# Masking the second-pass probabilities of key tile 3 on GpSimd instead of TensorE

## The reference

```python
h = relu(layernorm(x))
q, k, v = heads(h @ Wq + bq), heads(h @ Wk + bk), heads(h @ Wv + bv)
scores = einsum('bhqd,bhkd->bhqk', q, k) * scale
scores = where(adj[:, None] == 0, -inf, scores)
attn = softmax(scores, axis=-1)
x = x + einsum('bhqk,bhkd->bhqd', attn, v) @ Wo + bo
```

## Time and profile before

| | |
|---|---|
| median of 3 runs | 1721.32 us (1720.43 to 1723.81) |
| profiled execution, its own time | 1723.0 us |
| its span, first to last instruction | 1721.1 us |
| TensorE busy | 1661.3 us, 97% |
| VectorE busy | 1533.7 us, 89% |
| ScalarE busy | 1475.2 us, 86% |
| GpSimd busy | 146.1 us, 8% |
| mean granted clock of TensorE | 0.988 of full speed |

### The profile page before, as it was taken

One profiled execution on the slowest core, in us unless ns is written; L12 is line 12 of the kernel. 1 busy time (PEld: TensorE's weight loads), 2 busy tenths in 40 slices (PEclk: granted clock), 3 DMA queues, 4 the chain that ended last, 5 costly groups with the idle time before them and its releaser, 6 DMA issues.

```text
span 1721.1 us, 27544 instructions
## 1 busy us (share of the span) xinstructions
PE 1661.3 (97%) x8001; PEld 1037.7 (60%) x8001; DVE 1533.7 (89%) x3659; ACT 1475.2 (86%) x3497; POOL 146.1 (8%) x199
## 2 busy tenths in 40 slices
PE   6789999999999999999999999999999999999998
PEld 4546665665666666666665666666666666666643
DVE  5799998999989899898999989899898999989885
ACT  3699898888988989889898988989888888988975
POOL 0001100011010010100001000011100011010010
PEclk9799999999999999999999999999999999999989
DMA  6334343433433344343333433344343333433320
GB/s 189 97 90 110 99 108 83 117 90 110 112 99 111 82 117 111 99 106 87 115 91 108 115 92 113 85 117 112 99 105 85 113 93 109 113 97 100 88 76 25
DMA packets 117164, 175.15 MB, mean 102 GB/s; under 512 B 30860, under 2 KB 32920, under 8 KB 117016
## 3 DMA queue, kind: packets, MB, share of 16 engines
q1 hardware_dynamic: 112344, 171.56, 37.0%
q10 hardware_dynamic: 4672, 1.84, 0.5%
HBM read 54.79 MB, written 16.78 MB: 42 GB/s over the span
## 4 chain that ended last, share of the span: by engine, by line
PE 78%; DVE 15%; issue 3%; ACT 2%; ACTq 1%; DMA 0%; SPq 0%; DVEq 0%
PE ps L775 14%; PE psO L809 13%; PE psP L679 12%; PE psP L680 11%; PE ps L789 11%; PE psP L681 11%; DVE ps L572 5%; DVE probs L579 4%; PE ps L792 3%; PE ps L726 1%; DVE x_tile L491 1%; ACT ps L412 1%; DVE stats L483 1%; DVE neg_max L572 1%; DVE oT_lo L592 1%
## 5 line engine op out<-in xcount | busy, mean ns | idle before, releaser
L572 DVE CUSTOM_DVE_ANT_0 ps<-ps,bias_q 128x512 f32<-128x512 f32 x1024 | 708.7, 694 | 136.2 <-PE ps L775 126.8
L412 ACT ACTIVATE ps<-ps,neg_max 128x512 f32<-128x512 f32 x1024 | 686.7, 671 | 101.4 <-DVE neg_max L572 83.3
L448 ACT ACTIVATE probs<-ps 128x512 f32<-128x512 f32 x1024 | 621.3, 607 | 74.1 <-PE ps L792 69.7
L579 DVE SCALAR_TENSOR_TENSOR probs<-bias_k,probs 128x512 f32<-128x512 bf16 x768 | 552.4, 720 | 8.1 <-ACT probs L448 8.0
L775 PE MATMUL ps<-k_stack,q_stack 96*128 96x512 f32 x1024 | 451.7, 441 | 19.2 <-ACT ps L412 13.9
L789 PE MATMUL ps<-q_stack,k_stack 98*128 98x512 f32 x1024 | 410.7, 401 | 3.7 <-ACT probs L448 3.5
L775 PEld LDWEIGHTS ps<-k_stack,q_stack 96*128 96x128 f32 x1024 | 194.6, 190 | 276.2 <-ACT ps L412 135.5
L809 PE MATMUL psO<-probs,v_sb 128*32 128x512 f32 x2048 | 275.0, 609 | 2.1 <-DVE oT_lo L592 0.9
L789 PEld LDWEIGHTS ps<-q_stack,k_stack 98*128 98x128 f32 x1024 | 195.4, 191 | 40.5 <-ACT probs L448 15.7
L412 ACT ACTIVATION_READ_ACCUMULATOR ps<-ps,neg_max 128x1 f32 x1024 | 217.9, 213 | 0.0
L572 DVE DVE_READ_ACCUMULATOR2_ANT neg_max<- 128x1 f32 x1024 | 144.0, 141 | 0.0
(11 more groups left out here) (75 smaller groups left out, 1930.6 us busy)
## 6 DMA issues: line engine op xcount, KB each, us to landing
q_stack<-part_hi SPq DMA_DIRECT2D x512, 64.0 KB, 2.0
k_stack<-part_hi SPq DMA_DIRECT2D x504, 64.0 KB, 2.0
x_tile<-in_x_dram SPq DMA_DIRECT2D x64, 256.0 KB, 2.9
y_tile<-in_x_dram SPq DMA_DIRECT2D x64, 256.0 KB, 2.9
adj_tile<-in_adj_dram SPq DMA_DIRECT2D x64, 256.0 KB, 3.0
q_stack<-part_lo SPq DMA_DIRECT2D x256, 64.0 KB, 2.0
k_stack<-part_lo SPq DMA_DIRECT2D x252, 64.0 KB, 2.0
out_dram<-y_tile SPq DMA_DIRECT2D x62, 256.0 KB, 2.1
```

What stands on the lines that cost most here:

```text
L412: nc.scalar.activation(item, item, ACT.Exp, scale=-1.0, bias=neg_max[:, g % 2, col:col + 1], accum_out=exp_sum[:, col:col + 1]).then_inc(e ...
L448: nc.scalar.activation(probs[:, n % P_RING, :], ps2[:, n % 2, :], ACT.Exp, scale=SCALE).then_inc(exp2_done, 1)
L572: nc.vector.tensor_tensor_reduce(bank1(("s", u)), bank1(("s", u)), bias_q[:, qt, :], -SCALE, 3.0e38, ALU.add, ALU.min, neg_max[:, g % 2, c ...
L579: nc.vector.scalar_tensor_tensor(out=probs[:, n % P_RING, :], in0=bias_k[:, n % 16 // 4, :], scalar=-MASKED, in1=probs[:, n % P_RING, :], ...
```

## The change

The masks of pass 2 are divided by key tile. VectorE masks key tiles 0, 1 and 2 of every head group with the same instruction as before (12 of each 16 tiles in a row, then 4 not); GpSimd masks key tile 3 (n % 16 in 12 to 15) by an integer product of the probability's bits with a 0/1 tile `keep_k`; TensorE's mask matmul is gone. `bias_k` holds three key tiles instead of four; ScalarE writes key tile 3 from PSUM as `keep_k` (int32, 1 + bias / 2^100). The second turn of the mask moves from slot 61 to slot 62, and its move to SBUF is now two instructions, of which the second waits for all products of the graph before. GpSimd's small work is placed in slots among the products.

```diff
-VECTOR_MASKED = (0, 1, 2, 4, 5, 6)
+GPSIMD_KEY_TILES, VECTOR_KEY_TILES = (3,), (0, 1, 2)
...
-         24: [("c", 2, -1)], 40: [("c", 3, -1)], 53: [("m", 0, 0)], 56: [("c", 0, 0)], 61: [("m", 1, 0)]}
+         24: [("c", 2, -1)], 40: [("c", 3, -1)], 53: [("m", 0, 0)], 56: [("c", 0, 0)], 62: [("m", 1, 0)]}
...
+            def mask(b, n):
+                kt = n % 16 // 4
+                if n < 16 and n % 4 == 0:
+                    pool.wait_ge(m_done, due(2 * b + kt // 2 + 1))
+                pool.wait_ge(exp2_done, due(64 * b + n + 1))
+                tile = probs[:, n % P_RING, :].bitcast(I32)
+                nc.gpsimd.tensor_tensor(tile, tile, keep_k[:, GPSIMD_KEY_TILES.index(kt), :], ALU.mult).then_inc(gpsimd_masked, 1)
+
             def step(k, parity):
...
+                for u in range(SLOTS):
+                    if k > 0 and u == 5: form_rstd(k, 2)
+                    if k > 0 and u == 10: form_rstd(k, 3)
+                    if u == 12 and k - 2 != LAST: add_bo(k - 2, 3)
+                    b, n = pass2(k, u)
+                    if have(b) and n % 16 // 4 in GPSIMD_KEY_TILES:
+                        mask(b, n)
+                    if u == 8 and k - 2 != LAST: add_bo(k - 2, 2)
+                    if u in (43, 44): form_rstd(k + 1, u - 43)
+                    if u in (49, 50): add_bo(k - 1, u - 49)
+                    if u in (52, 53) and k - 1 == LAST: add_bo(LAST, u - 50)
...
+                            turned = bank1((kind, n, rel)).bitcast(BF16)
+                            act.wait_ge(vector_masked, due(VECTOR_ALL * (k - 1) + masked_before(48 + 8 * n + 8, VECTOR_KEY_TILES)))
+                            if n == 0:
+                                nc.scalar.activation(bias_k[:, 0:2, :], turned.rearrange("p (t q) -> p t q", q=S), ACT.Identity).then_inc(m_done, 1)
+                            else:
+                                nc.scalar.activation(bias_k[:, 2, :], turned[:, 0:S], ACT.Identity).then_inc(bias_k_done, 1)
+                                act.wait_ge(gpsimd_masked, due(GPSIMD_ALL * k))
+                                nc.scalar.activation(keep_k[:, 0, :], turned[:, S:2 * S], ACT.Identity,
+                                                     scale=-1.0 / MASKED, bias=1.0).then_inc(m_done, 1)
...
-                    if have(b) and n % 8 in VECTOR_MASKED:
+                    if have(b) and n % 16 // 4 in VECTOR_KEY_TILES:
...
-                        last = nc.tensor.matmul(ps2[:, n % 2, :], k_stack[:, g, j, P * kt:P * kt + P], q_stack[:, g, j, :],
-                                                start=True, stop=(n % 8 in VECTOR_MASKED))
-                        if n % 8 not in VECTOR_MASKED:
-                            last = nc.tensor.matmul(ps2[:, n % 2, :], ident_b[:], bias_k[:, kt, :], start=False, stop=True)
-                        last.then_inc(scores2, 1)
+                        nc.tensor.matmul(ps2[:, n % 2, :], k_stack[:, g, j, P * kt:P * kt + P], q_stack[:, g, j, :],
+                                         start=True, stop=True).then_inc(scores2, 1)
...
-                        pe.wait_ge(probs_masked, due(MASKED_ALL * b + masked_before(4 * n + 4)))
+                        if kt in VECTOR_KEY_TILES:
+                            pe.wait_ge(vector_masked, due(VECTOR_ALL * b + masked_before(4 * n + 4, VECTOR_KEY_TILES)))
+                        else:
+                            pe.wait_ge(gpsimd_masked, due(GPSIMD_ALL * b + masked_before(4 * n + 4, GPSIMD_KEY_TILES)))
```

38 lines of the change are left out of this document (13 added, 25 removed).

## The result

The changed kernel takes 1761.28 us (median of 4 runs, 1757.05 to 1762.83) against 1722.57 for the kernel before on the same chip (4 runs, 1720.43 to 1725.91): ratio 1.0224, 95% interval 1.0207 to 1.024. The forecast was 1707 us, the range ended at 1738: wrong in direction and outside the range. The profiled execution has a span of 1760.8 us, 39.7 more than before.

The account below looks back on a forecast made before the run. It took TensorE's list to bound the kernel nearly everywhere, VectorE close behind: 58.9 us gross, less 43.5 (2.9 in each of fifteen blocks) and 1.3 once, gains 14.1 us. Forecast 1707 us, range 1672 to 1738.

Parts of the forecast that it names:

- gross gain: TensorE loses 256 mask matmuls at 0.23 us each: 58.9 us in all, 3.7 us per block.
- bunching: Twelve mask-heavy slots in a row, then four light; in slots 14 to 21 VectorE has 12.96 us against TensorE's 11.80.
- slots 2-13 (1st group): GpSimd's products and small work delay slot 14's PV product and normalisation L491: 0.9 us per block, bounds 0.3 and 2.5.
- slots 14-21: Eight VectorE masks instead of six put it 1.2 us behind, mostly absorbed: 0.3 us charged, bounds 0 and 1.2.
- borders / slots 38-45: GpSimd's products meet VectorE's masks where light slots begin, half of three borders hit: 0.3 us per block.
- slots 46-53: VectorE's 12.90 us plus 1.2 us of masks; 13.4 us taken, bounds 12.5 and 14.1: 0.9 us charged.
- slots 54-1 (turn): ScalarE's split mask move, one slot later, delays attention output and output projection: 0.5 us per block, bounds 0 and 1.
- tail, once: At the very end the last product stands between the last exponential and last PV product: 1.3 us once.
- VectorE as the bound: Rival: eight products per block each cost a mask or L491 1.2 us, VectorE needs 104.3 us; 1732 us, chance 0.15.
- The slow integer product: Rival: GpSimd's product takes over about 1.6 us; at 2.0 us 1738, at 2.6 us near 1840; chance 0.15.
- the gain is kept: Rival: VectorE's light slots absorb the charges, only about 0.8 us per block is lost: 1676 us, chance 0.25.
- Masks of 1.2 to 1.8 us at the borders only: Sign of being right: VectorE's masks stretched only at borders; stretched masks inside groups would show the forecast wrong.

Follow-up runs that it names:

- e12: The kernel before the change with GpSimd's bias additions cut to one column (the rest of the bias left out): 1700.7 us, ratio 0.9879.
- e9: e6 with the masks divided in the old order, GpSimd on every fourth tile (3 and 7 of 8), some mask tiles wrong: 1661.59 us, ratio 0.9646.
- e3: The changed kernel with the second turn of the mask back in slot 61: 1739.9 us, ratio 1.0103.
- e4: The changed kernel with GpSimd's bias additions on one column instead of 512: 1719.92 us, ratio 0.9983.
- e7: The changed kernel with the turn in slot 61 and the bias additions of slots 49 and 50 moved to 57 and 58: 1713.29 us, ratio 0.995.
- e2: The changed kernel with GpSimd's products on one column instead of 512: 1727.39 us, ratio 1.0044.
- e1: The kernel before with masks divided by key tile, key tile 3 staying on TensorE, no product on GpSimd: 1756.76 us, ratio 1.0201.
- e6: The changed kernel with GpSimd's products and bias additions on one column and the turn back in slot 61: 1690.72 us, ratio 0.9822.
- e5: The changed kernel with both GpSimd's products and its bias additions on one column: 1706.7 us, ratio 0.9918.

## Why the prediction was wrong, step by step

The gross gain was right for the quiet stretches: 0.23 us per matmul, 5.88 us per four slots as forecast. But even without locks, bunching and moved turn only 39 of the 58.9 us arrive (e12 to e9). The charges against the full gain were 2.9 us per block and measured 6.0 (each is the mean stretch after, less the mean stretch before and its full gain):

```
                      forecast  measured
slots 2-13 (1st group)   0.9      1.12
slots 14-21              0.3      0.44
borders / slots 38-45    0.3      0.51
slots 46-53              0.9      1.95
slots 54-1 (turn)        0.5      1.95 (1.37 of it the turn, e3)
tail, once               1.3      8.7 (5.0 longer, and the 3.7 of its own gain gone)
```

The 3.1 us more in each of 15 blocks and the 7.4 more in the tail are 54 us, the whole miss from 1707 to 1761.

**The step that failed first: slots 46 to 53.** The prediction added 1.2 us of masks to VectorE's 12.90 and took 13.4, "nearer to VectorE's row because nothing was absorbed before". The mean is 14.68, above even the upper bound. Bunching explains 0.4 of the 1.95 us: with the additions short or elsewhere the stretch takes 13.10 (e4 to e7). What failed is the term for the addition's lock, which it held to be "in these numbers" already. Its row (rows 5) has one addition in the stretch, and the other 2.1 us ahead. It did not ask where the new products would push GpSimd's old work: into the stretch, where the first addition makes VectorE late and the second meets the normalisation, in 11 of 15 blocks. e12 has this lock at 0.46 us per block, e2 at 0.57, the changed kernel at 1.58. A lock is not a constant that can be carried from one schedule to the next; it depends on what is met. How much VectorE's missing slack adds by itself is not separated; between e12 and e2 it is 0.1 us, though e1, with bunched masks and its additions placed as before, has some 0.9 (14.04 less 13.10, an estimate).

**The second: the turn.** The prediction charged 0.5 us, bounds 0 and 1, from ScalarE's own time for the moves. What counted was their place in an in-order list: the moves wait for a turn that TensorE starts only after its PV product, and the exponential and the high part behind them wait as well. The stretch 62-1 became 1.31 us longer in two blocks of three. Nor was it foreseen that in the others the granted clock falls as well (+1.58 us). e3 and e6 put the whole at 16 to 21 us; 7.5 were charged. That the wait lowers the clock is not shown by a run of its own. It is argued from what comes just ahead, and from e6 and e7, which have neither the wait nor a lowered clock there.

**The third: bunching.** It was seen (12.96 against 11.80 us in slots 14 to 21) and "most of it is absorbed" was right for those slots (0.16 us, e9 to e6). It costs 29 us (e9 to e6) in places that had no term for it or too small a one: slots 2 to 9 (0.60 us), 38 to 45 (0.46), 46 to 53 (0.48) and the tail (5.75 once).

**Right in size by luck: the first group.** The charge was 0.9 us and measured 1.12, but the prediction let the PV product of slot 14 wait for GpSimd's chain. It waits in none of the 15 blocks: the last product is done 0.7 to 2.3 us ahead of it. TensorE's hole in slots 10 to 13 is a wait of 0.6 us per block for the exponential L421, against 0.2 us in e5. And the working's line that L522 at 412.07 is not stretched shows nothing, since no 128x512 instruction of GpSimd was under way then; that it is not stretched is shown by other rows (below).

**The rivals.** The second, VectorE as the bound (1732 us), is nearest to the case that came, though not as it was built and 29 us too low: its price was eight products each meeting a mask. In fact 54 of the 768 masks and 18 of the 62 normalisations take over 0.8 us, all of them in the first group, in slots 46 to 53 and in the last block; the full-length instructions cost 9.4 us in the tail besides (92.21 to 82.76 in e5). It had a chance of 0.15, too low for an engine at 12.90 of 12.97 us. The slow integer product had as much and was wrong: 1.31 us. That the gain is kept did not come true in any run: with short products and additions, the old order and the old turn, 39 of 58.9 us are left of it.

Of the signs named ahead, these came: 5.88 us, products of 1.27 to 1.71 us, VectorE without idle time and TensorE with holes in slots 46 to 53. "Masks of 1.2 to 1.8 us at the borders only" did not: 1217.44 and 1226.73 lie inside. The Trainium skill's rule ("SBUF — State Buffer", SBUF: two separate sides), by which a lock is held for a whole instruction, agrees with the stretched rows shown here (the mask of 1226.73 runs on until 0.55 us behind the addition's end). What a lock costs the kernel, and that was the error, had to come from the schedule.

## What to carry to other kernels

When a change puts new work into an engine's list, look at where it pushes the old work of that list, and what the old work will meet there: in slots 46 to 53 the same two additions cost 0.46 us per block before, 0.57 with the products cut short and 1.58 behind full ones, when they met the normalisation. Look at how masks, or whatever is shared out, follow one another, not only at how many there are: the order alone was worth 29 us without locks (e9 to e6) and 35 in the kernel before (e1). And a gain that is worked out for the bounding engine must be set against the second one stretch by stretch: of 58.9 us 39 arrived with nothing else in the way (e12 to e9). Last, before an eviction is moved by one slot, read what stands behind it in the in-order list of its engine and who waits for that.
